# Six matmul steps of the last down block move behind the turnings of y back, and loads of B in front of stores

## What is computed

```python
x = L0_attn_hidden_states                       # (2, 1024, 512)
xn = _layernorm(x)
# branch s: x, z = split(xn @ in_proj_w); xc = silu(conv(x)); dt = softplus(...)
#   per state n of 16:  h = exp(dt*A[:, n]) * h_prev + dt*xc * B[n]   (a scan over 1024)
#   y = sum_n h * C[n];   y = (y + D*xc) * silu(z);   s = y @ out_proj_w.T
# branch g: h = silu(gate(xn)) * up(xn);  g = silu(down(h))
x = x + s * g
```

## Time and profile before

| | us |
|---|---|
| runs | 1307.87, 1303.16, 1305.86; median 1305.86 |
| profiled execution | 1304.8 |
| its span | 1303.0 |
| busy PE / DVE / ACT / POOL | 1170.5 / 998.1 / 705.7 / 729.1 |
| POOL ub L529, share of the chain that ended last | 26% |
| PE down L903, share of that chain | 8% |

### The profile page before, as it was taken

The page is one execution under the profiler, slowest core; times in us unless marked ns, Lnnn a source line. Parts: engine busy times, 40 slices in busy tenths (PEclk is TensorE's granted clock), DMA queues, the critical chain, the costliest instruction groups (busy, mean ns, idle before and its releaser), DMA issues.

```text
span 1303.0 us, 12893 instructions
## 1 busy us (share of the span) xinstructions
PE 1170.5 (90%) x4414; PEld 611.9 (47%) x4414; DVE 998.1 (77%) x822; ACT 705.7 (54%) x870; POOL 729.1 (56%) x406
## 2 busy tenths in 40 slices
PE   4997869999997999998999885999999699999898
PEld 2433335555543555555444332555554355555543
DVE  2886499999859999995405439999985999999531
ACT  2212757777664777772013374777765477777200
POOL 2000079999704899991220006999881289999311
PEclk9998879999998999999999987999999899999999
DMA  7453218999842699987611111799985149999841
GB/s 224 165 180 129 72 41 203 230 212 244 196 124 77 156 232 218 240 204 220 238 41 40 40 46 59 189 228 210 237 202 149 64 131 229 215 234 217 239 162 40
DMA packets 60643, 214.27 MB, mean 164 GB/s; under 512 B 6330, under 2 KB 6458, under 8 KB 60196
## 3 DMA queue, kind: packets, MB, share of 16 engines
q0 software_dynamic: 16128, 88.09, 35.1%
q1 hardware_dynamic: 42868, 119.70, 26.7%
q10 hardware_dynamic: 1584, 5.68, 1.2%
HBM read 102.39 MB, written 22.98 MB: 96 GB/s over the span
## 4 chain that ended last, share of the span: by engine, by line
PE 36%; POOL 31%; DVE 16%; issue 7%; DMA 6%; ACT 2%; SPq 0%; POOLq 0%; DVEq 0%; ACTq 0%
POOL ub L529 26%; PE psA L753 8%; PE psM L903 8%; PE psM L952 8%; DVE hb L1103 6%; POOL yT L539 4%; PE psT L881 4%; DMA bn<-ss_rows_scratch 4%; PE psA L855 2%; DMA yT<-yc 2%; PE psM L779 2%; DVE dtx L977 2%; DVE dt L1085 1%; DVE th L977 1%; PE psM L800 1%
## 5 line engine op out<-in xcount | busy, mean ns | idle before, releaser
L529 POOL TENSOR_TENSOR ub<-dtx,bn 128x1024 f32<-128x1024 f32 x256 | 640.8, 2556 | 407.7 <-issue 249.2
L1103 DVE TENSOR_TENSOR_SCAN hb<-psA,ub 128x1024 f32<-128x1024 f32 x256 | 579.7, 2279 | 22.6 <-POOL ub L529 10.2
L779 PE MATMUL psM<-xnT,w_ts 128*126 128x512 f32 x704 | 353.3, 632 | 41.7 <-DVE hid L977 25.7
L647 ACT ACTIVATE psA<-dt,cc 128x1024 f32<-128x1024 f32 x256 | 286.5, 1119 | 172.2 <-DVE hb L1103 137.2
L881 PEld LDWEIGHTS psT<-ident,hb 128*128 128x128 f32 x2048 | 236.0, 142 | 209.9 <-issue 88.3
L881 PE MATMUL psT<-ident,hb 128*128 128x128 f32 x2048 | 286.8, 279 | 43.7 <-DVE yT L977 29.0
L666 ACT ACTIVATE yc<-psT,ssm 128x512 f32<-128x512 f32 x336 | 217.3, 678 | 49.6 <-PE psT L881 49.6
L779 PEld LDWEIGHTS psM<-xnT,w_ts 128*126 128x126 f32 x704 | 129.0, 201 | 163.6 <-issue 131.6
L903 PE MATMUL psM<-w_dn,hid 126*128 126x512 f32 x352 | 167.9, 606 | 0.0
L977 DVE SCALAR_TENSOR_TENSOR yT<-psT,ssm,yT 128x512 f32<-128x512 f32 x144 | 105.1, 736 | 54.9 <-PE psT L881 33.3
L893 PE MATMUL psM<-xnT,w_ts 128*128 128x512 f32 x256 | 119.1, 593 | 0.0
(11 more groups left out here) (83 smaller groups left out, 649.7 us busy)
## 6 DMA issues: line engine op xcount, KB each, us to landing
yT<-yc POOLq DMA_DIRECT2D x112, 768.0 KB, 7.2
bn<-ss_rows_scratch SPq DMA_DIRECT2D x64, 512.0 KB, 6.3
w_ts<-w_gu_scratch SPq DMA_DIRECT2D x44, 504.0 KB, 4.4
w_ts<-w_in_dram SPq DMA_DIRECT2D x32, 256.0 KB, 4.5
z_scratch<-th SPq DMA_DIRECT2D x32, 256.0 KB, 4.6
hb<-z_scratch SPq DMA_DIRECT2D x16, 512.0 KB, 9.8
w_gu_scratch<-hid ACTq DMA_DIRECT2D x11, 504.0 KB, 4.4
yT<-x_dram SPq DMA_DIRECT2D x2, 2048.0 KB, 12.7
```

The lines of the kernel that those rows point to most:

```text
L529: pool.tensor_tensor(ub[:, i % 2, :], dtx[:, i, :], bn[:, t, :], ALU.mult).then_inc(s_u, 1)
L647: act.activation(psA[:, i % 2, :], dt[:, i, :], ACT.Exp, scale=negA[:, h * DH + i, bass.ds(n, 1)]).then_inc(s_a, 1)
L779: mm = pe.matmul(psM[0:IM, gu, :], w_ts[:, t, at:at + IM], xnT[:, k, h * CH:(h + 1) * CH], start=(k == 0), stop=(k == HK - 1))
L1103: dve.tensor_tensor_scan(hb[:, t * DH + i, :], psA[:, i % 2, :], ub[:, i % 2, :], 0.0, ALU.mult, ALU.add).then_inc(s_scan, 1)
```

## The change

In every half, the steps of the late states are dealt out so that 66 steps fill the first 28 quarters, as before in number, and each quarter of the last state has one step, four in all; six steps of the last down block (j = 3, k = 5 to 10) remain. Behind the first half they stand two each behind the first three turn_backs, and the new half's `gate_up` of block 0, until now cut up between the turn_backs, comes behind the fourth (`ahead(0)`). Behind the second half they stand three each behind the first two turn_backs, in front of the out_part there. The tanh and the product of that block move with them (`late_end`, and `silu_late` behind the first half's `finish_y(2)` or the second's `finish_y(1)`), and the `lost` of VectorE's passage comes one place forward. ScalarE's wait for the stores of the half before, which stood at the start of the second half, now stands in front of its `ahead(0)`, behind the logs. In `SP_LATE` the loads of B come forward.

```diff
@@ -64,10 +64,15 @@
 STEPS = [("z", i, s) for i in range(DH) for s in range(2 * HK)] + [("d", j, s) for j in range(CH // P)
                                                                   for s in range(IT)]
 QUARTERS = 4 * (NS - LATE)
+REST = 6
+INSIDE = len(STEPS) - REST - 4
 def steps_of(p):
-    return STEPS[len(STEPS) * p // QUARTERS:len(STEPS) * (p + 1) // QUARTERS]
+    if p < QUARTERS - 4:
+        return STEPS[INSIDE * p // (QUARTERS - 4):INSIDE * (p + 1) // (QUARTERS - 4)]
+    return STEPS[INSIDE + p - QUARTERS + 4:INSIDE + p - QUARTERS + 5]
 def ends(p):
@@ -83,10 +88,11 @@
-SP_LATE = [("B", 8), ("Z", 0), ("B", 9), ("Z", 1), ("B", 10), ("z", 0, 0), ("Z", 2), ("z", 0, 1), ("B", 11),
-           ("z", 1, 0), ("Z", 3), ("z", 1, 1), ("B", 12), ("z", 2, 0), ("z", 2, 1), ("B", 13), ("z", 3, 0),
-           ("z", 3, 1), ("G", 0), ("G", 1), ("B", 14), ("d", 0, 0), ("B", 15), ("w",), ("d", 1, 0), ("back",), ("W",), ("d", 2, 0),
-           ("d", 3, 0)]
+SP_LATE = [("B", 8), ("B", 9), ("Z", 0), ("B", 10), ("Z", 1), ("B", 11), ("z", 0, 0), ("Z", 2), ("z", 0, 1),
+           ("B", 12), ("z", 1, 0), ("Z", 3), ("z", 1, 1), ("z", 2, 0), ("B", 13), ("z", 2, 1), ("z", 3, 0),
+           ("B", 14), ("z", 3, 1), ("G", 0), ("G", 1), ("B", 15), ("d", 0, 0), ("d", 1, 0), ("w",), ("back",), ("W",),
+           ("d", 2, 0), ("d", 3, 0)]
 T_ACT = TB + 2
@@ -670,7 +676,7 @@
                         tanh_gate(n, n % 2)
-                    def tanh_late(kind, i, c):
+                    def late_end(h, kind, i, c):
                         t = c if kind == "z" else i % 2
                         if kind == "d":
@@ -687,9 +693,13 @@
                             act.wait_ge(s_ths[t], th_stored(b, h, (i if kind == "z" else DH + i // 2) - 1))
                         act.activation(th[:, t, :], psM[:, t, :], ACT.Tanh, scale=0.5).then_inc(s_th, 1)
-                    for t in range(2):
-                        act.wait_ge(s_ths[t], th_stored(b, h, -1))
+                    def tanh_late(kind, i, c):
+                        late_end(h, kind, i, c)
                     if h == 0:
+                        for t in range(2):
+                            act.wait_ge(s_ths[t], th_stored(b, h, -1))
                         ahead(0)
                         for i in range(DH):
                             relu_abs(0, i)
@@ -697,10 +707,14 @@
                         one_plus_exp(h, i)
                         if h == 0 and i == 1:
                             ahead(1)
+                    if h:
+                        late_end(0, "d", JD - 1, 0)
                     act.wait_ge(s_dtr, blk(b, h, DH))
                     for i in range(DH):
                         log(h, i)
                     if h:
+                        for t in range(2):
+                            act.wait_ge(s_ths[t], th_stored(b, h, -1))
                         ahead(0)
                     for i in range(DH):
                         act.wait_ge(s_dt, blk(b, h, i) + 1)
@@ -731,8 +745,7 @@
                             if p % 4 > 1:
                                 one_plus_exp(h + 1, p % 4 - 2)
                             relu_abs(h + 1, p % 4)
-                    for what in ends(QUARTERS - 1):
-                        tanh_late(*what)
+                late_end(HALVES - 1, "d", JD - 1, 0)
                 if b + 1 < NB:
                     layer_norm(b + 1)
@@ -922,7 +935,9 @@
                     else:
                         for i in range(DH):
                             turn_back(i)
-                            gate_up(b, h, 0, w_half(h, 0) % 2, i, landed(b, w_half(h, 0)))
+                            for kind, j, step in STEPS[len(STEPS) - REST:][2 * i:2 * i + 2]:
+                                down(j, step)
+                        ahead(0)
                     for n in range(1, FILL):
                         ahead(n)
                     for n in range(LATE):
@@ -957,6 +972,9 @@
                 pe.wait_ge(s_wo, 16 * b + 16)
                 for i in range(DH):
                     turn_back(i)
+                    if i < 2:
+                        for kind, j, step in STEPS[len(STEPS) - REST:][3 * i:3 * i + 3]:
+                            down(j, step)
                     out_part(i // 2, range(i % 2 * 2, i % 2 * 2 + 2))
                 for tb in range(2):
                     out_part(tb, range(DH, DB))
@@ -1127,7 +1145,7 @@
                         dve.wait_ge(s_mf, m_half(b, h, 2 * n) + 3)
                         stt(hid[0:IM, n, :], th[0:IM, t, :], 0.5, psM[0:IM, 1, :], ALU.mult, ALU.mult).then_inc(s_mf, 1)
-                    def silu_late(kind, i, c):
+                    def silu_late(h, kind, i, c):
                         t = c if kind == "z" else i % 2
                         dve.wait_ge(s_th, th_done(b, h, kind, i, c))
@@ -1147,6 +1165,8 @@
                     if h == HALVES:
                         for i in range(DH):
                             finish_y(i)
+                            if i == 1:
+                                silu_late(HALVES - 1, "d", JD - 1, 0)
                         break
                     if h == 0:
                         silu_gate(0, 0)
@@ -1170,10 +1190,11 @@
                     else:
                         lost(1, 1)
                         finish_y(0)
+                        lost(1, 2)
                         finish_y(1)
-                        lost(1, 2)
+                        lost(1, 3)
                         finish_y(2)
-                        lost(1, 3)
+                        silu_late(0, "d", JD - 1, 0)
                         finish_y(3)
                         drive(0)
                         silu_gate(0, 0)
@@ -1203,15 +1224,13 @@
                             add_y(n, Y_ORDER[2 * q])
                         if p:
                             for what in ends(p - 1):
-                                silu_late(*what)
+                                silu_late(h, *what)
                         if by_dve(n, Y_ORDER[2 * q + 1]):
                             add_y(n, Y_ORDER[2 * q + 1])
                         if p == 0:
                             hidden(IT - 1, (IT - 1) % 2)
                     if h + 1 < HALVES:
                         lost(h + 1, 0)
-                    for what in ends(QUARTERS - 1):
-                        silu_late(*what)
                 dve.wait_ge(s_gl, 16 * b + 16)
                 for tb in range(TB):
```

## The result

The changed kernel takes 1322.8 us (median of four runs, 1317.8 to 1324.2) against 1304.5 for the kernel before (four runs, 1303.1 to 1307.9; the three given above and a fourth): ratio 1.0122, interval 1.0103 to 1.0141. The forecast was 1303.5. The profiled execution took 1324.2, its span 1322.3.

What follows compares the result with a forecast made beforehand. No engine was taken to bind throughout (TensorE 36% and GpSimd 31% of the chain led), so stages were read singly. The terms summed to -2.5 us, from the median 1305.86 to a forecast of 1303.5, range 1298.0 to 1309.5.

Steps and rivals of the forecast that it cites:

- Term 1: Late states: B loads issued before stores remove TensorE's gaps, -6.9 us in first halves and -2.4 in second halves.
- Term 2: First half's last state: the last turn comes four steps earlier, -6.9 us over both batches.
- Term 3: Passage to second half: gate matmuls behind all four turn_backs make tanh_gate(0,0) late, +2.4 us, bounds 0 and +7.6.
- three signs of being wrong: VectorE waiting over 3 us at silu_gate(0,0), a B load over 10 us, or second-half steps in idle time behind turn_back.
- Terms 4, 5 and 6: End of second half: 4, earlier turn_back(0) -1.6, six more steps +10.3; 5, late g_scratch +1.0; 6, slower TensorE clock +1.6 us.
- Cold TensorE: Passage and second half's end: idle TensorE gets 1.2 GHz, gate 3.8 us late; +5.1 in all, 1311.0; chance 0.09.
- The loads are no sooner: Late states: traffic, not queue place, makes B loads long, so nothing is gained there; +6.8 us, 1312.7; chance 0.05.

Runs made afterwards that it cites:

- e1: Kernel before with only the new SP_LATE, loads of B in front of stores: 1304.0 us, ratio 0.9978.
- e2: Changed kernel with the old SP_LATE, so only the steps moved: 1322.9 us, ratio 1.0120.
- e4: e3 with the second half's last ten steps as before the change, none behind its turn_backs: 1294.9 us, ratio 0.9901.
- e5: e4 with the old SP_LATE, stores in front of B again: 1301.4 us, ratio 0.9939.
- e3: Changed kernel with the second half's B loads for states 0 and 1 issued before the weight loads: 1307.1 us, ratio 1.0012.
- e7: Kernel before with the second half's B loads for states 0 and 1 in front of the weight loads: 1307.0 us, ratio 0.9998.
- e10: Changed kernel with two gate quarters of gate_up(0) back between the turn_backs, B's loads unaltered: 1315.6 us, ratio 1.0069.
- e6: e5 with B for state 14 before the last z store and two weight loads, entries behind it as in the change: 1294.6 us, ratio 0.9895.
- e9: e6 with the two gate quarters of gate_up(0) back between the turn_backs: 1295.9 us, ratio 0.9908.

## Why the prediction was wrong, by its own steps

*Term 1, B in front of stores* (-6.9 in the first halves, -2.4 in the second): mis-sized. "The stores become ready at nearly the same moments, so the stores lose little" is where it failed. They are issued as early as before (the first z store of e1 115.5 behind the first scan, 115.4 before), but right behind 512 KB of B in the same queue, and land after 8.6 us instead of 4.6; ScalarE waits for `th`, its copies come late, and TensorE waits for those. The first halves had most of their part, 5.9 in e1 and 5.2 from e2 to the changed kernel; the second halves had nothing of theirs in e1 and lost 4.0 in the other pair. In time e1 measured 1.9 to 2.9 for the whole term, e4 against e5 about 5, where I had 9.3.

*Term 2, four steps less before the last turn* (-6.9): right. The steps alone made the first halves 7.4 shorter up to the last addition (e2), and on top of the new order 6.8 (e1 to the changed kernel).

*Term 3, the passage* (+2.4, bounds 0 and +7.6): this is the step that failed. The wait at silu_gate(0,0) was sized well, 1.52 and 0.64 against 1.2, though in e3, where nothing hides it, it moved the first scan by only 0.8 in both batches together. But I listed for gate_up(0) only those who need its result, ScalarE and VectorE, and not SyncE, which needs its buffer. Behind SyncE's wait stand the loads of B for states 0 and 1. I had looked at SyncE's queue in the late states and at its end, and not behind it, at the head of the second half. The passages lost 12.5 instead of 2.4. e3 gave 15.7 us of the whole back by the order of these loads alone; e7 shows that this order is worth nothing without the moved gate; e10 moved the end of gate_up(0) and B went with it. The upper bound was false too, since it knew only this one waiter. And none of the prediction's three signs of being wrong came: the wait for tanh was 1.52, the longest load of B took 9.6, and the six steps didn't fall into idle time. They stood where I already looked for trouble.

*Terms 4, 5 and 6, the end of the second half* (-1.6 +10.3 +1.0 +1.6 = +11.3): right. e4 against e3 measured 12.2. turn_back(0) began when w_out landed in both batches, and g_scratch came 0.7 and 0.5 late. The lower clock came in the first batch alone (0.69 granted over 7.5 us, three steps in 4.17; in the second they took 2.74), so that term's 0.8 a batch is right only as a mean of the two.

*Rivals.* "Cold TensorE" had the right sign and a small part: the low clock of the first passage held block 0's buffer 1.7 us longer, and through the queue B. But it isn't what made the loss. e3 leaves TensorE's program as it is, one of its two passages ran at the lower clock too, and it is level with the kernel before. "The loads are no sooner" fell: GpSimd's waits went.

*The sum.* With term 1 at the -2.9 of e1 instead of -9.3 and term 3 at +15.7 plus the 2.2 of the gate (1.52 and 0.64), the terms give -2.9 -6.9 +15.7 +2.2 +11.3 = +19.4; measured were 18.3 between the medians, 15.9 by the ratio. That is no independent check, since the 15.7 is itself the changed kernel less e3. What it leaves to check is e3: the other terms give +3.7 against the kernel before, and measured were +1.2, with an interval from -1.2 to +4.2.

## What to carry to other kernels

When a step moves, list every engine that waits for its end, the one that refills its buffer as well as those that use its result, and for each what is queued behind that wait. Work put into an engine's room is free only in a place where that engine isn't itself the path: the same six steps cost next to nothing in the first half's passage (e4 and e6 have them there, and from the last addition to the first scan it is 26.2 or 26.3, where it was 26.1 and 26.6) and cost their full time at the end of the second. And a small store behind a large load in one queue can pay for the load: here a store of 256 KB took 8.6 us instead of 4.6.

## What the runs showed of the hardware

The stretch up to the first scan has the same code in all kernels, and its length went with the clock that TensorE was granted, if not closely. These are the windows 130:150 of the kernel after and of e3; the first scan came at 169.7 and 166.0.

```profile
130.00:150.00 20.00, 19.28 (x28) 0.66 0.19 52
```

```profile
130.00:150.00 20.00, 17.89 (x41) 0.91 0.21 65
```

In e9's execution 0.59 was granted there and the first scan came at 170.7, but with 0.83 in this window it came anywhere from 166.1 to 168.8. Profiled executions differ by up to 4.8 us in this place alone (166.0 to 170.7), a good 0.3% of the whole, with no edit near it. Two single profiles should therefore be compared from mark to mark and not by their ends.
